# One 128-partition DMA for dt's broadcast, and C's column copies and two normalisations on ScalarE, in a Mamba block on one core

## What is computed

```python
def step(h, ins):                       # h: [8, E, N]
    x_t, dt_t, B_t, C_t = ins
    dA = jnp.exp(dt_t[..., None] * A)   # A: one number for each of the N states
    h = dA * h + dt_t[..., None] * B_t[:, None, :] * x_t[..., None]
    y_t = jnp.einsum('ben,bn->be', h, C_t)
    return (h, y_t)
h0 = jnp.zeros((Bsz, E, N), x.dtype)
_, y = jax.lax.scan(step, h0, (xc.transpose(1, 0, 2), dt.transpose(1, 0, 2), Bp.transpose(1, 0, 2), Cp.transpose(1, 0, 2)))
y = y.transpose(1, 0, 2) * jax.nn.silu(z)
x = x + y @ out_proj_W
n2 = rmsnorm(x, ffn_norm_w)
ffn = jax.nn.silu(n2 @ gate_W) * (n2 @ up_W) @ down_W
return x + ffn
```

## Time and profile before

| | |
|---|---|
| median of 3 runs | 2097.97 us (2094.41 to 2103.18) |
| profiled execution | 2099.65 us, its span 2097.5 us |
| busy share of the span | TensorE 60%, VectorE 49%, ScalarE 42%, GpSimd 41% |
| DMA, mean of 16 engines | 72.6% for the queue of SP's DMAs, 321 MB, 153 GB/s over the span |
| mean granted TensorE clock | 0.674 |

### The profile page before, as it was taken

How to read it: one execution, slowest core, us unless ns; L and a number is a source line. 1 busy time by engine, 2 the same in 40 slices (tenths; PEclk the granted TensorE clock), 3 DMA queues, 4 the chain that set the end, 5 groups by cost and what they waited for, 6 DMA issues and landing times. The chain is left out here.

```text
span 2097.5 us, 27406 instructions
## 1 busy us (share of the span) xinstructions
PE 1261.5 (60%) x8012; PEld 501.4 (24%) x8012; DVE 1017.5 (49%) x2237; ACT 875.7 (42%) x964; POOL 849.6 (41%) x1215
## 2 busy tenths in 40 slices
PE   6990246666555565566555665666655566576558
PEld 3560011222211222122211222122211222122224
DVE  4762255555454445455444444455443445455444
ACT  3772244444343434344433433344433434344442
POOL 4541244444343343444333343444343344344342
PEclk9995555666677667676657556676575666666677
DMA  2227588788778687878878687878878787878871
GB/s 88 98 98 163 120 181 174 159 169 173 165 161 164 151 169 159 164 161 159 172 155 162 149 169 149 170 157 161 171 157 164 144 167 164 160 157 160 168 161 34
DMA packets 97938, 321.18 MB, mean 153 GB/s; under 512 B 9056, under 2 KB 22240, under 8 KB 95456
## 3 DMA queue, kind: packets, MB, share of 16 engines
q1 hardware_dynamic: 97760, 319.12, 72.6%
HBM read 303.37 MB, written 15.73 MB: 152 GB/s over the span
## 5 line engine op out<-in xcount | busy, mean ns | idle before, releaser
L863 POOL TENSOR_TENSOR decayed<-decay,state 128x256 f32<-128x256 f32 x1024 | 725.5, 731 | 1127.0 <-DVE state L1163 1081.1
L1099 ACT ACTIVATE decay<-decay,a_col 128x2048 f32<-128x2048 f32 x256 | 514.0, 2008 | 1002.4 <-DMA decay<-dt_stage 983.8
L1152 DVE TENSOR_TENSOR ps<-decay,ps 128x512 f32<-128x512 f32 x512 | 353.4, 690 | 860.6 <-ACT state L1111 762.7
L917 PE MATMUL ps<-moving,b_rows 36*128 36x256 bf16 x1024 | 264.2, 351 | 752.5 <-DVE ps L1152 734.3
L972 PE MATMUL ps<-state,c_cols 128*32 128x256 f32 x4096 | 460.0, 533 | 0.3 <-issue 0.3
L1163 DVE TENSOR_TENSOR state<-decayed,ps 128x256 f32<-128x256 f32 x1024 | 387.6, 415 | 96.8 <-PE ps L972 58.5
L1111 ACT COPY state<-ps 128x512 f32<-128x512 f32 x512 | 281.7, 583 | 112.1 <-issue 58.7
L917 PEld LDWEIGHTS ps<-moving,b_rows 36*128 36x128 bf16 x1024 | 62.7, 101 | 997.2 <-DVE ps L1152 665.4
L924 PE MATMUL ps<-moving,b_rows 36*128 36x256 bf16 x1024 | 265.4, 352 | 33.0 <-DMA b_rows<-b_stage 33.0
L1057 PE MATMUL ps<-h,w 128*128 128x256 f32 x512 | 238.5, 562 | 0.9 <-DVE h L1285 0.8
L1057 PEld LDWEIGHTS ps<-h,w 128*128 128x128 f32 x512 | 105.7, 252 | 144.1 <-issue 140.1
(11 more groups left out here) (115 smaller groups left out, 883.0 us busy)
## 6 DMA issues: line engine op xcount, KB each, us to landing
decay<-dt_stage SPq DMA_DIRECT2D x256, 1024.0 KB, 14.7
moving<-u_stage SPq DMA_DIRECT2D x64, 288.0 KB
b_rows<-b_stage SPq DMA_DIRECT2D x256, 36.0 KB
dt_stage<-dt_tok SPq DMA_DIRECT2D x8, 512.0 KB, 2.6
u_stage<-u_parts SPq DMA_DIRECT2D x8, 512.0 KB, 2.8
b_stage<-b_parts SPq DMA_DIRECT2D x8, 384.0 KB, 2.8
u_stage<-u_parts SPq DMA_DIRECT2D x8, 256.0 KB, 2.0
x_in<-in_L_attn_x_dram SPq DMA_DIRECT2D x32, 64.0 KB
```

Of the source, the lines that this page charges most:

```text
L863: nc.gpsimd.tensor_tensor(decayed[:, p], decay[:, dec_slot(m, k), p, k % TS, :], state[:, (k - 1) % RING, p * E:(p + 1) * E], ALU.mult).th ...
L917: return nc.tensor.matmul(ps[:, acc_bank(m, k), p * E:(p + 1) * E], b_rows[rows(1), cb, p, kk, :], moving[rows(1), cb, kk, :], start=False ...
L1099: nc.scalar.activation(pair, pair, ACT.Exp, scale=a_col[:, 2:3]).then_inc(decay_ready, 1)
L1152: nc.vector.tensor_tensor(ps[:, acc_bank(m, k), :].rearrange("p (q e) -> p q e", q=HQ), decay[:, dec_slot(m, k), HQ:Q, k % TS, :], ps[:, a ...
```

## The change

dt_stage in DRAM becomes [2 halves, 128 chunks, 4 q, 4 steps, E], so that what a chunk needs of one half lies in one run of 16 KB. load_dt issues one DMA for the whole slot; its source is [2, 64, 4096] and its destination the 128 partitions. The semaphore counts 16 for each chunk. place_c moves from VectorE to ScalarE as it is (the first chunk's ahead of the scan, the second's at step 4, the others after copy_state at the same step as before). Of the output stage, the normalisation of x becomes an activation on ScalarE with a scale and a bias; the bias, -mean * rstd, is a new small product on VectorE (K_SHIFT), and the steps K_STATS to K_XN are set anew. The scaling by the root mean square becomes an activation on ScalarE at its old step.

```diff
@@ -55,7 +55,7 @@
     NACC = 3
     BTS = STEPS // TS
     CYCLE = 3
-    assert CYCLE * BTS % NDEC == 0 and CYCLE * STEPS % NACC == 0
+    assert TS == NJ and CYCLE * BTS % NDEC == 0 and CYCLE * STEPS % NACC == 0
 
     TG = STEPS
     NG = T // TG
@@ -65,7 +65,7 @@
 
 
     u_stage = nc.dram_tensor("u_stage", (2, NP, HALF, T, E), BF16, kind="Internal").ap()
-    dt_stage = nc.dram_tensor("dt_stage", (2, Q, T, E), F32, kind="Internal").ap()
+    dt_stage = nc.dram_tensor("dt_stage", (2, T // TS, Q, TS, E), F32, kind="Internal").ap()
     b_stage = nc.dram_tensor("b_stage", (NP, B, T, 2 * N), BF16, kind="Internal").ap()
 
     with ExitStack() as ctx:
@@ -258,7 +258,7 @@
                         n = q * 2 + bb
 
                         wait_all(sp, [(S["dt_ready"], n + 1)])
-                        sp.dma_start(dt_stage[bb, q].rearrange("(p j) e -> p (j e)", j=NJ),
+                        sp.dma_start(dt_stage[bb, :, q].rearrange("p j e -> p (j e)"),
                                      dt_tok[:, bb].rearrange("p j e -> p (j e)")
                                      ).then_inc(S[f"dt_stored{bb}"], 16)
                         for parts, stage, i0, i1, ready in (
@@ -626,7 +626,7 @@
             y_tok = pb("y_tok", [P, GT, E])
             f_stats = pb("f_stats", [P, GT, 6])
             f_mv = pb("f_mv", [P, GT, 2])
-            f_nrm = pb("f_nrm", [P, 4, GT])
+            f_nrm = pb("f_nrm", [P, 5, GT])
             square = pb("square", [P, GT, D])
             sumsq = pb("sumsq", [P, GT])
             xn = pb("xn", [P, GT, D])
@@ -640,7 +640,7 @@
             h2 = pb("h2", [P, H2 // P, GTOK])
             gate = pb("gate", [P, IH, GTOK])
             result = pb("result", [P, GT, D])
-            names = ("f_x_loaded f_stats_ready f_mv_ready f_rstd_ready f_xn_ready f_xn_t_ready f_xn_feat_ready "
+            names = ("f_x_loaded f_stats_ready f_mv_ready f_rstd_ready f_shift_ready f_xn_ready f_xn_t_ready f_xn_feat_ready "
                      "f_y_t_ready f_gated_ready f_proj_ready f_x1_ready f_sumsq_ready f_rrms_ready f_n2_ready "
                      "f_n2_t_ready f_n2_feat_ready f_h1_proj f_h1_ready f_h2_proj f_h2_ready f_gate_ready "
                      "f_gate_tanh_ready f_silu_ready f_up_ready f_hid_ready f_sum_ready f_base "
@@ -651,7 +651,7 @@
 
 
 
-            K_STATS, K_MOMENTS, K_RSTD_SUM, K_RSTD, K_XN, K_XN_T, K_XN_FEAT = -5, -4, -3, -2, -1, 2, 3
+            K_STATS, K_MOMENTS, K_RSTD_SUM, K_RSTD, K_SHIFT, K_XN, K_XN_T, K_XN_FEAT = -7, -6, -5, -4, -2, 0, 2, 3
             K_Y_T, K_GATED, K_OUT, K_X1, K_SQUARE, K_RRMS_SUM, K_RRMS, K_BASE, K_N2 = 6, (7, 8), 9, 11, 12, 13, 15, 18, 17
             K_N2_T, K_N2_FEAT = 19, 20
             K_GATE, K_GATE_TANH, K_SILU, K_UP, K_HID = 22, 24, (25, 26), (30, 32), 33
@@ -747,14 +747,13 @@
             with nc.Block() as block:
                 @block.sync
                 def _(sp):
-                    def load_dt(t, slot, waits):
+                    def load_dt(c, slot, waits):
 
                         wait_all(sp, waits)
-                        for bb in range(2):
-                            sp.dma_start(decay[bb * N:(bb + 1) * N, slot].rearrange("n q t e -> n q (t e)"),
-                                         dt_stage[bb, :, bass.ds(t, TS), :].rearrange("q t e -> q (t e)")
-                                         .unsqueeze(0).broadcast_to([N, Q, TS * E])
-                                         ).then_inc(dt_loaded[slot], 16)
+                        sp.dma_start(decay[:, slot].rearrange("n q t e -> n (q t e)"),
+                                     dt_stage[:, bass.ds(c, 1)].rearrange("b c q t e -> b (c q t e)")
+                                     .unsqueeze(1).broadcast_to([2, N, Q * TS * E])
+                                     ).then_inc(dt_loaded[slot], 16)
 
                     def load_u(t, cb, waits):
 
@@ -779,8 +778,8 @@
                     load_dt(0, 0, [])
                     load_u(0, 0, [])
                     load_b(0, 0, range(B))
-                    load_dt(TS, 1, [])
-                    load_dt(2 * TS, 2, [])
+                    load_dt(1, 1, [])
+                    load_dt(2, 2, [])
                     load_u(TC, 1, [])
                     load_b(TC, 1, range(B))
                     for dst, src in ((k0_raw, k0), (k1_raw, k1), (k2_raw, k2)):
@@ -808,7 +807,7 @@
                             if last and kc + 2 >= BTS:
                                 return
                             used = t0 + kc * TS
-                            load_dt(t0 + (kc + 2) * TS, (m * BTS + kc + 2) % NDEC,
+                            load_dt(i * BTS + kc + 2, (m * BTS + kc + 2) % NDEC,
                                     [(self_state[1], used)] if waiting else [])
 
                         first = known(i) and i == 0
@@ -1094,9 +1093,17 @@
                             return
                         slot, ts = dec_slot(m, k), k % TS
                         if ts == 0:
-                            act.wait_ge(dt_loaded[slot], dec_loads(m, r, k) * (16 * 2))
+                            act.wait_ge(dt_loaded[slot], dec_loads(m, r, k) * 16)
                         pair = decay[:, slot, :, ts:ts + 2, :].rearrange("p q t e -> p q (t e)")
                         nc.scalar.activation(pair, pair, ACT.Exp, scale=a_col[:, 2:3]).then_inc(decay_ready, 1)
+
+                    def place_c(chunk, cb):
+
+                        for bb in range(2):
+                            m = nc.scalar.copy(
+                                c_cols[bb * N:(bb + 1) * N, cb, :, bb * TC:bb * TC + (TC - 1) * (2 * TC + 1) + 1:2 * TC + 1],
+                                cb_feat[bb * N:(bb + 1) * N, bb, :, bass.ds(chunk * TC, TC)])
+                        m.then_inc(c_placed, 1)
 
                     def copy_state(i, k, m):
 
@@ -1117,9 +1124,28 @@
                             exp_decay(i, k + 2, m, r)
                             copy_state(i, k - 2, m)
                             copy_state(i, k - 1, m)
+                        if known(i) and i == 0 and k == 4:
+                            place_c(1, 1)
+                        chunk = i * 2 + k // TC
+                        if k % TC == LAG + 8 and not (known(i) and i == 0 and k < TC or known(chunk) and chunk == NC - 1):
+                            place_c(chunk + 1, (k // TC + 1) % 2)
                         finish_groups(finish, i, k)
 
                     def finish(g, k):
+                        if k == K_XN:
+                            after(act, "f_shift_ready", g)
+                            act.wait_ge(G["f_x_loaded"], (g + 1) * (16 * GT))
+                            after(act, "f_x1_ready", g, back=1)
+                            for j in range(GT):
+                                m = nc.scalar.activation(xn[:, j], x_in[:, j], ACT.Identity, bias=f_nrm[:, 4, j:j + 1],
+                                                         scale=f_nrm[:, 1, j:j + 1])
+                            m.then_inc(G["f_xn_ready"], 1)
+                        if k == K_N2:
+                            after(act, "f_rrms_ready", g)
+                            after(act, "f_n2_t_ready", g, back=1)
+                            for j in range(GT):
+                                m = nc.scalar.activation(n2[:, j], x1[:, j], ACT.Copy, scale=f_nrm[:, 3, j:j + 1])
+                            m.then_inc(G["f_n2_ready"], 1)
                         if k == K_SQUARE:
                             after(act, "f_x1_ready", g)
                             after(act, "f_rrms_ready", g, back=1)
@@ -1133,6 +1159,7 @@
                             nc.scalar.activation(gate[:].rearrange("p h t -> p (h t)"), ps[:, FA, :], ACT.Tanh,
                                                  scale=0.5).then_inc(G["f_gate_tanh_ready"], 1)
 
+                    place_c(0, 0)
                     chunks(act, step)
                     copy_state(BODIES - 1, STEPS - 2, (BODIES - 1) % CYCLE)
                     copy_state(BODIES - 1, STEPS - 1, (BODIES - 1) % CYCLE)
@@ -1164,8 +1191,6 @@
                                                     ps[:, SELFP + k % 2, p * E:(p + 1) * E], ALU.add
                                                     ).then_inc(self_state[p], 1)
 
-                        if k % TC == LAG + 8 and not (known(t) and t < TC or known(chunk) and chunk == NC - 1):
-                            place_c(chunk + 1, (k // TC + 1) % 2)
                         if known(i) and i == 0:
                             binary_weights(k)
                         finish_groups(finish, i, k)
@@ -1189,14 +1214,6 @@
                             nc.vector.tensor_scalar(w2[:], w2[:], s_fold[:, 1:2], None, ALU.mult).then_inc(bin_ready, 1)
                         if k == 20:
                             nc.vector.tensor_scalar(w1[:], k1_raw[:], 2.0, -1.0, ALU.mult, ALU.add).then_inc(bin_ready, 1)
-
-                    def place_c(chunk, cb):
-
-                        for bb in range(2):
-                            m = nc.vector.tensor_copy(
```

(21 more changed lines are left out.)

## The result

The changed kernel takes 5717.66 us (median of 4 runs, 5716.24 to 5718.53); the kernel before takes 2096.19 us beside it. The ratio is 2.728, 95% interval 2.718 to 2.738. The profiled execution has a span of 5714.4 us.

A forecast was written before the change was run, and what follows sets the result against it. The prediction took the DMA loads, chiefly dt, as the bound: 178 + 5478 (dt) + 356 (u) + 178 (B) + 33 + 44 = 6267 us, with 2 us around the span 6269, say 6270; range 5870 to 8600 us.

The forecast's parts named there:

- The loads set the pace: Scan before the change: a four-step chunk waits at best 10.2 us for dt, against 4 us of exponentials.
- The merged load runs on two engines: New dt load: its source counts 2 outermost, so it runs on two of 16 DMA engines; chance 0.63 at about 25 GB/s each.
- Rate of an engine: New dt load: two engines carry 49 GB/s together, so 128 loads take 128 x 42.8 = 5478 us.
- The fast bound: Range's low end, 5870 us: dt at 25.6 GB/s an engine (5235 us), u and B at their fastest.
- u, B, x, start and tail: Terms beside dt: u 356, B 178, x_in and out 33, before the first dt load 178, tail 44 us.
- The queue never runs dry: DMA queue in the scan: the next dt load is always queued, so waits behind large loads cost nothing; otherwise up to 224 us.
- The moved work is covered: Copies and normalisations moved to ScalarE: 39 to 61 us, hidden while it waits for dt; up to 61 us if uncovered.
- Rival 1: New dt load: two engines at u's 17.7 GB/s each, 8374 us; chance 0.25, with rates between.
- Rival 2: New dt load: spread over all 16 engines, the 64-partition limit lifted; 1537 us, down to 1300; chance 0.10.
- Rival 3: New dt load: 16 engines still at 205 GB/s, limited by repeated reading of one source; 2100 us; chance 0.02.

The follow-up runs named there:

- e5: Changed kernel with dt stored twice in DRAM, so the merged load's source counts 4 outermost; 3319 us.
- e6: Changed kernel with dt stored four times in DRAM, so the merged load's source counts 8 outermost; 2746 us.
- e4: Changed kernel with dt stored 8 times over in DRAM, so the merged load's source counts 16 outermost; 1900.74 us, ratio to the kernel before 0.908.
- e7: Changed kernel with four merged dt loads of 4 KB pieces for each chunk, one for each q, source still counting 2 outermost; 5807.5 us.
- e9: As e7, but with the kernel before's layout of dt in DRAM, a chunk's four rows 512 KB apart; 5804.8 us.
- e1: Kernel before with the merged dt load alone, plus the layout and semaphore count it needs; column copies and normalisations stay on VectorE; 5717.08 us.
- e10: Changed kernel with one 16 KB row of dt copied to all 128 partitions, 128 outermost; second batch half gets the first's dt; 1463.5 us.
- e12: As e10, but each of the 128 partitions reads its own 16 KB DRAM row, from other chunks, so dt is wrong; 1467.3 us.
- e3: Changed kernel with its new dt layout, but again two DMAs of 64 partitions for each chunk; 2020.49 us, ratio to the kernel before 0.963.
- e8: As e3, but the load of the upper 64 partitions is issued from ScalarE's own queue; 2071.18 us, ratio to the kernel before 0.986.

## Why the prediction was right in its mechanism and wrong in its number

- **The loads set the pace.** Right: the wait that led before leads after.
- **The merged load runs on two engines.** Right, and shown: a share of 0.13, and 0.25, 0.51 and 1.00 in e5, e6 and e4 as the outermost count is raised to 4, 8 and 16.
- **Rate of an engine.** This is the step that failed. Take the forecast's other terms as they stand, and dt had 5714 - 178 - 567 - 44 = 4925 us, 38.5 us for each of 128 chunks, or 54.5 GB/s, against 42.8 us at 49 GB/s. Long windows with dt alone in flight read 54:

```profile
708.00:778.00 70.00, 17.60 (x98) 5.38 (x98) 9.94 (x21) 8.24 (x15) 11.62 (x18) 0.52 0.13 54
```

  At 54 GB/s dt takes 128 x 38.8 = 4971 us. The term of 5478 us was 507 us too large, some nine tenths of the miss (6270 to 5717.66). I had taken 49 GB/s from a window of 2 us at the tail of a queue. 98 KB are only 24 pieces of 4 KB, and one piece more or less is worth 4%. Other tails of the same kernel show how coarse such a window is:

```profile
730.00:732.00 2.00, 0.00 (x0) 0.00 (x0) 0.34 (x1) 2.00 (x4) 0.00 (x0) 0.50 0.13 53
1200.00:1202.00 2.00, 0.00 (x0) 0.00 (x0) 0.34 (x1) 2.00 (x4) 0.00 (x0) 0.50 0.12 43
```

  Whether two engines are also a little slower in a tail than in steady work isn't shown. e7 and e9 have 53 GB/s in 30 us with the same pieces, e9 with the same rows.
- **The fast bound.** It was 25.6 GB/s an engine from a half microsecond of a store, and loads do 27. I let the fastest row seen be the end of the range, with nothing for the coarseness of a short window. At 25.6 dt was still 5235 - 4971 = 264 us too long. u and B at their best took off another 157 us, more than they should have, and that wasn't enough. Some 3% more on dt's bound would have held the result.
- **u, B, x, start and tail.** Start (178 us) and tail (43) stayed. With dt at 4971 us, 5714 - 178 - 43 - 4971 = 522 us are left for u, B, x and out, against 567 in the sum and 410 with u and B at their best. This rests on the windows' whole GB/s: 1 GB/s more or less moves it by some 90 us.
- **The queue never runs dry.** Right: 0.14 over 5300 us of the scan, and VectorE's wait for x_in behind the last chunk's load (630 us, 16 times) is there as described. It costs nothing: e1, where the statistics of x stand at their old steps, has no such wait and takes the same time.
- **The moved work is covered.** Right beside the merged load (e1 against the change: 0.6 us). ScalarE's groups after, forms apart:

```profile
L1103 ACT COPY c_cols<-cb_feat 64x64 f32 x48 | 14.7, 306 | 0.3
L1140 ACT ACTIVATE xn<-x_in,f_nrm 128x128 f32<-128x128 f32 x32 | 14.3, 506 | 0.0
L1147 ACT ACTIVATE n<-x,f_nrm 128x128 f32<-128x128 f32 x32 | 11.4, 419 | 1.4 <-POOL f_nrm L886 1.4
```

  The column copy takes 306 ns, the low end of its bounds. The normalisations take 506 and 419 ns, not the square's 307. The sum, 14.7 + 4.9 for the copies' other form + 14.3 + 11.4 = 45 us, lies within 39 to 61.
- **Rival 1** (u's 17.7 GB/s an engine) fell: a load on few engines isn't slow by itself, nor are long pieces. The earlier trace rows was also a slow row for u: of the kernel before, 61 windows of 2 us (230 to 1850 us, end to end) have a share of 0.18 to 0.20, and they read 66 GB/s on average, 22 an engine. Why it had 17.7 there wasn't tried.
- **Rival 2** fell with the two engines, but its price was sound where its condition holds: e10 and e12 take 1464 and 1467 us, between its 1300 and 1537. It would not have come from 16 engines alone: e4 has them and takes 1901.
- **Rival 3** describes e3 and e8, 16 engines at 210 to 215 GB/s, but not for the reason it gave; e10 reads one row 128 times at 428.

## What to carry to other kernels

Before merging two DMAs, read the outermost count of both sides of the new one: here a source that counts 2 outermost left two of 16 DMA engines at work, 54 GB/s for 205, and made the kernel 2.7 times as long. A mean DMA share that stands at a multiple of a sixteenth (0.13, 0.19, 0.25, 0.5) is the sign of it, and it was in the trace before, in the loads of u. When a forecast multiplies one rate 128 times, take the rate from the longest window there is, and widen the range by what a short window can't resolve.

## What the runs showed of the hardware

- The number of DMA engines of a load goes with the outermost count of its source: 2, 4, 8, 16 give a share of 0.13, 0.25, 0.51, 1.00 (e1 and the change, e5, e6, e4).
- The rate doesn't go with it: 54, 104, 121, 214 GB/s for the same 2 MB to the same 128 partitions, and up to 430 once the source counts 128 outermost, as long as no u load is in flight beside it (some 230 then, in e10 and e12). Eight engines (e6) carry 16% more than four (e5).
- Reading one 16 KB row 128 times is as fast as reading 128 rows (428 and 430 GB/s, 1463.5 and 1467.3 us).
- Two queues with a half each (e8) move no more than one queue with both (e3): 210 and 215 GB/s at a full share. In e8 the two halves mostly went one after the other all the same; the two longest stretches in which they were mixed (3.5 and 3.3 us) had 204 GB/s.
